# Twelve buffers in place of six for the expert blocks' results

## What is computed

```
gates = softmax(xf @ router_w);  top_v, top_i = top_k(gates, 2)
masked = top_v placed at top_i, divided by its sum
routed[e] = silu(rmsnorm(xf) * rms_w[e] @ w1[e]) @ w2[e]       # e = 0..13, 128 -> 256 -> 128
out = x + sum_e masked[:, e] * routed[e] + two shared experts of the same shape
```

## Time and profile before

| | us |
|---|---|
| median of 3 runs | 412.38 (411.79 to 412.67) |
| profiled execution, its own time | 412.95 |
| its span, first to last instruction | 411.2 |
| POOL's first send of the expert blocks begins | 261.4 |
| SP starts the first load of the results | 391.5 |

### The profile page before, as it was taken

One profiled execution on the slowest core, in us unless ns is written; L12 is line 12 of the kernel. 1 busy time (PEld: TensorE's weight loads), 2 busy tenths in 40 slices (PEclk: granted clock), 3 DMA queues, 4 the chain that ended last, 5 costly groups with the idle time before them and its releaser, 6 DMA issues.

```text
span 411.2 us, 9224 instructions
## 1 busy us (share of the span) xinstructions
PE 281.8 (69%) x2810; PEld 248.4 (60%) x2810; DVE 222.1 (54%) x837; ACT 167.3 (41%) x339; POOL 174.6 (42%) x231
## 2 busy tenths in 40 slices
PE   1945765559666768556656499969797879779800
PEld 1944654558454646354556398969686869678700
DVE  7999977972376455735653041353434343434374
ACT  1466486756485335543541132432323233232300
POOL 2793000008006447445647300355565655646540
PEclk9995798969996598889857599999999998999965
DMA  6750089997000111011102132122222232222289
GB/s 172 254 239 0 17 232 262 266 328 194 0 2 32 33 40 47 32 33 47 40 32 66 60 78 54 33 74 73 72 65 73 63 78 66 77 68 72 65 305 307
DMA packets 54577, 41.67 MB, mean 101 GB/s; under 512 B 6248, under 2 KB 50941, under 8 KB 54033
## 3 DMA queue, kind: packets, MB, share of 16 engines
q1 hardware_dynamic: 47552, 31.60, 26.8%
q0 software_dynamic: 4544, 8.47, 6.5%
q10 hardware_dynamic: 2448, 1.20, 1.1%
HBM read 29.14 MB, written 13.02 MB: 103 GB/s over the span
## 4 chain that ended last, share of the span: by engine, by line
PE 25%; DVE 25%; another core or an unknown queue 16%; issue 12%; DVEq 7%; DMA 5%; ACT 5%; SPq 4%; ACTq 0%
PE bank L1493 4%; DVEq L960 4%; PE bank L1581 3%; PE bank L1592 3%; PE bank L1474 2%; DVE u L698 2%; PE bank L1370 2%; PE bank L1416 2%; DVE area L980 2%; DMA area<-kp_dram 2%; ACT v L1059 2%; PE bank L1293 2%; PE bank L1306 1%; DVE stats L649 1%
## 5 line engine op out<-in xcount | busy, mean ns | idle before, releaser
L588 POOL DMA_INDIRECT y_dram<-area,ybi x78 | 77.9, 998 | 87.8 <-DVE area L980 70.5
L582 POOL DMA_INDIRECT xs_dram<-area x64 | 63.0, 984 | 64.5 <-issue 39.3
L961 DVE COPY v<-v 128x512 f32 x84 | 37.1, 441 | 31.0 <-issue 31.0
L1581 PE MATMUL bank<-xn,v 128*128 128x128 f32 x320 | 44.6, 282 | 3.5 <-DVE v L961 1.8
L1592 PE MATMUL bank<-v,xn 128*128 128x128 f32 x312 | 42.6, 281 | 5.4 <-ACT xn L1240 5.4
L1581 PEld LDWEIGHTS bank<-xn,v 128*128 128x128 f32 x320 | 38.9, 192 | 7.6 <-DVE v L961 4.0
L1592 PEld LDWEIGHTS bank<-v,xn 128*128 128x128 f32 x312 | 38.8, 195 | 6.4 <-DVE area L980 5.2
L1240 ACT ACTIVATE xn<-bank 128x512 f32<-128x512 f32 x40 | 24.1, 602 | 33.0 <-PE bank L1581 20.1
L979 DVE COPY ybi<-area 128x2 uint32<-128x2 uint32 x39 | 7.0, 181 | 54.6 <-remote 40.0
L1235 ACT COPY xn<-bank 128x256 f32<-128x256 f32 x41 | 15.1, 371 | 45.5 <-remote 25.0
L1474 PE MATMUL bank<-v 128*128 128x128 f32 x160 | 26.5, 313 | 9.2 <-issue 9.2
(11 more groups left out here) (298 smaller groups left out, 641.6 us busy)
## 6 DMA issues: line engine op xcount, KB each, us to landing
area<-kp_dram SPq DMA_DIRECT2D x12, 512.0 KB, 6.8
area<-xs_dram SPq DMA_DIRECT2D x84, 65.0 KB
area<-y_dram SPq DMA_DIRECT2D x8, 512.0 KB, 7.6
x_sb<-in_L_attn_x SPq DMA_DIRECT2D x4, 512.0 KB, 8.0
area<-ab_dram SPq DMA_DIRECT2D x2, 1024.0 KB, 6.1
xn<-ab_dram SPq DMA_DIRECT2D x2, 1024.0 KB, 10.9
xn<-kp_dram SPq DMA_DIRECT2D x4, 512.0 KB, 6.8
out_x<-x_sb SPq DMA_DIRECT2D x8, 256.0 KB, 6.5
```

Of the source, the lines that this page charges most:

```text
L582: pool.indirect_dma_start(out=xs_dram.ap(), out_offset=bass.IndirectOffsetOnAxis(ap=pos[:, k, i:i + 1], axis=0), in_=hx[:, i, k, :], in_of ...
L588: pool.indirect_dma_start(out=y_dram.ap(), out_offset=bass.IndirectOffsetOnAxis(ap=ybi[:, z:z + 1].bitcast(U32), axis=0), in_=yb[:, z, :], ...
L961: v.tensor_copy(wc[:, z % STEP], v1_flat.rearrange("p (w m) -> p w m", w=2)[:, :, bass.ds(r, HID)]).then_inc(wc_ready, 1)
L1581: last = mm(bank[2 + p % 2][:, HID * j + P * c:HID * j + P * c + P], wc[:, (2 * p + j) % STEP, 1, P * c:P * c + P], xsT[:, p % 3, P * j:P ...
```

## The change

`yb`, `ybi`, `yb_out`, `last_of` and `ltab` get UNROLL = 12 entries in place of six. `yb` and `ybi` move to a free part of the tensor `u`. POOL's sends take the slots in turn over twelve. DVE's expert loop becomes six pairs written out, a loop of five rounds of six pairs, and three pairs written out, again 39; from pair 6 on it waits for the sends of pair n - 6 (66 waits for 33 pairs). The additions of the shared experts stay at the same pairs. SP reads twelve values of `ltab` in three calls of four in place of six in one, and waits for twelve semaphores; at its end it waits for all twelve again.

```diff
-        yb = area[:, 11032:11032 + STEP * D].rearrange("p (z c) -> p z c", z=STEP)
+        yb = u_flat[:, 1088:1088 + UNROLL * D].rearrange("p (z c) -> p z c", z=UNROLL)
-        ybi = sb("ybi", [P, STEP])
+        ybi = u_flat[:, 2640:2640 + UNROLL]
-        last_of = sb("last_of", [P, STEP])
-        ltab = sb("ltab", [P, STEP], U32)
+        last_of = sb("last_of", [P, UNROLL])
+        ltab = sb("ltab", [P, UNROLL], U32)
-        yb_out = [sem(f"yb_out{z}") for z in range(STEP)]
+        yb_out = [sem(f"yb_out{z}") for z in range(UNROLL)]
             sp.wait_ge(ltab_ready, 1)
-            _, written = nc.values_load_multi_w_load_instructions(
-                ltab[0:1, 0:STEP], engines=[mybir.EngineType.SP], min_val=16 * (ROUTES // P // STEP), max_val=16 * (NBLK // STEP))
+            written = []
+            for z in range(0, UNROLL, 4):
+                written += nc.values_load_multi_w_load_instructions(
+                    ltab[0:1, z:z + 4], engines=[mybir.EngineType.SP], min_val=16 * (ROUTES // P // UNROLL),
+                    max_val=16 * (LOOPS + 1))[1]
             for z, r in enumerate(written):
                 sp.wait_ge(yb_out[z], r)
...
-            for z in range(STEP):
-                sp.wait_ge(yb_out[z], 16 * (NBLK // STEP))
+            for z in range(UNROLL):
+                sp.wait_ge(yb_out[z], 16 * (LOOPS + (z < STEP)))
...
-                    send_block(z % STEP)
+                    send_block((STEP + z) % UNROLL)
...
             def finish_pair(q, p):
-                row, z = 2 * p % UNROLL, 2 * p % STEP
+                row = z = 2 * p % UNROLL
...
+            def finish_again(q, p, sent):
+                for j in range(2):
+                    dve.wait_ge(yb_out[2 * p + j], sent)
+                finish_pair(q, p)
+
+            for p in range(STEP):
+                finish_pair(p, p)
+                if p == STEP - 1:
+                    add_looped(SH_FIRST)
+            with dve.Fori(0, LOOPS - 1) as it:
+                for p in range(UNROLL // 2):
+                    finish_again(it * (UNROLL // 2) + (STEP + p), p, it * 16 + 16)
+                    if p % 3 == 2:
+                        add_looped(it * SH_LOOP + (SH_FIRST + 1 + p // 3))
             for p in range(STEP // 2):
-                finish_pair(p, p)
-            with dve.Fori(0, LOOPS) as it:
-                for p in range(UNROLL // 2):
-                    for j in range(2):
-                        dve.wait_ge(yb_out[(2 * p + j) % STEP], it * (16 * UNROLL // STEP) + 16 * (1 + (2 * p + j) // STEP))
-                    finish_pair(it * (UNROLL // 2) + (STEP // 2 + p), STEP // 2 + p)
-                    if p % 3 == 2:
-                        add_looped(it * SH_LOOP + (SH_FIRST + p // 3))
+                finish_again((LOOPS - 1) * (UNROLL // 2) + STEP + p, p, 16 * LOOPS)
+            add_looped(NT - 1)
```

More of the change, by code:

```diff
@@ L946, in _ @@
             v.tensor_scalar(btab[0:1, :], bank[1][0:1, 2 * P:2 * P + LOADS], float(NULL), None, ALU.min)
-            v.tensor_scalar(last_of[0:1], iota_e[0:1, 0:STEP], cnb[0:1, E - 1:E], -1.0 / STEP, ALU.subtract, ALU.mult)
+            v.tensor_scalar(last_of[0:1], iota_e[0:1, 0:UNROLL], cnb[0:1, E - 1:E], -1.0 / UNROLL, ALU.subtract, ALU.mult)
             v.drain()
             v.engine_nop().then_inc(btab_ready, 1)
-            v.tensor_scalar(last_of[0:1], last_of[0:1], (STEP - 1) / STEP - 0.5 + 1.0 / (2 * STEP), MAGIC, ALU.add, ALU.add)
+            v.tensor_scalar(last_of[0:1], last_of[0:1], (UNROLL - 1) / UNROLL - 0.5 + 1.0 / (2 * UNROLL), MAGIC, ALU.add, ALU.add)
             v.drain()
```

## The result

The changed kernel takes 415.23 us, the median of 14 runs, against 412.33 us of the kernel before, also 14 runs. The ratio is 1.0059, with a 95% interval from 1.0035 to 1.0083: slower by 2.4 us (2.9 by the medians). Forecast were 414.8 us and +0.6%.

The account below looks back on a forecast made before the run. The prediction took the loop to be bound by PE's news arriving behind POOL's bursts of sends, not by landings, and SP's end to be on the path. 2.74 - 0.49 + 0.19 = +2.44; 412.38 + 2.4 = 414.8 us, range 412.3 to 416.9.

Parts of the forecast that it names:

- The waits: DVE before a pair's first instruction: the 40.0 us unknown wait is for PE's product, so twelve slots give 0 us.
- The estimate of 349.6 us: Landing of pair 24's second send, by the skill's DMA figures: 2.3 us before DVE asked for it.
- the order in the chain: Before line 979 on DVE: both landing waits were passed when the 2.63 us unknown wait began.
- ScalarE's simultaneous release: ACT, which waits for nothing from POOL's sends, was released at 354.68, 0.02 us ahead of DVE, after 4.77 us.
- the 21 ns: DVE's first landing wait, line 990: 21 ns in all 36 executions, taken to show that it never held.
- The rival from the semaphore rule: DVE's loop: PE's news costs only 56 ns, so landings held DVE; 21 us less in the loop, 393.8 us; chance 6%.
- SP's end: Between last row loads and first result load: two more calls 2.74, smaller first call -0.49, six more waits 0.19; +2.44 us.
- 1.5 to 3.5: Allowed growth in us from SP's last row load to first result load; outside it the end's price is wrong.
- Nothing hidden behind it: After SP's first result load: loads, additions and stores form one chain, so a later start moves everything, lengths unchanged.
- DVE's longer code and the other slots: DVE's 15 written-out or looped pair bodies (9 before), other buffer places and POOL's slot order: 0 us.
- Rival 4: Expert loop: bursts fall otherwise, winning or losing up to 3.9 us; faster, 410.9, 4%; slower, 418.7, 4%.

Follow-up runs that it names:

- the second pair of profiles: The unchanged kernel before and the changed twelve-slot kernel, both run again on chip 12: 413.66 and 414.07 us by the medians, ratio 1.0043.
- half of the sends: Kernel before, with POOL sending only each pair's even block and the waits for the odd block's landing left out; chip 12, one run: 380.18 us.
- the long end: SP's twelve values in three calls and twelve waits, as in the change; alone on the six-buffer kernel before, chip 11: 415.80 against 412.67 us, ratio 1.0095.
- early reading: SP's table reading moved ahead of its loop, chip 11: kernel before (six buffers) 410.01 us, ratio 0.9938; changed kernel (twelve) 411.65 us, 0.9960.
- sends to nowhere: Kernel before, every result row number out of bounds, so POOL executes all sends and no result is written; chip 12, one run: 412.19 us.

## Why the prediction was right

- *The waits.* Right: DVE's unknown waits aren't waits for landings. The change left them as they were (40.0 and 40.7 us, in the second pair of profiles 37.1 and 44.8), half of the sends removed them, and by the recorded times the landings came 2.3 us or more ahead of DVE's wait. The estimate of 349.6 us for the landing of pair 24's second send was good: its last semaphore update is at 349.59. Of the three reasons given, the order in the chain and ScalarE's simultaneous release were good ones, the 21 ns weren't.
- *The rival from the semaphore rule* of the Trainium skill ("TensorE: Matmul & The Clock Gate", "The cost: per-tile semaphore tail") fell: 56 ns doesn't hold while POOL works off sends; the news came 4 us late in the earlier trace rows. On chip 10 it came at most 0.02 us after the end of PE's row (which is modelled), so there is no such lateness there.
- *SP's end.* The sum was +2.44; the stretch grew by 2.0 and 2.8 us. The mechanism was right, all of it SP's own work on the path. The total was right with its parts uneven. In the first profile the table took 1.6 us more (2.25 forecast) and the waits 0.8 more (0.19 forecast), since one of the 0.7 us pauses fell among them, and the rows' DMAs gave back 0.4. The sum took the two pauses in the old table load as given and put none into what was added, because the new loads don't come right behind DMA starts. That reason doesn't hold: pauses fall on any instruction while POOL sends (last section). Their number differs from run to run, four, seven and nine in the stretches of 9.8, 10.5 and 11.9 us. Growths of 2.0, 2.8 and 4.1 us in three profiles with the long end mean that hitting +2.4 to the tenth was luck; the third lies outside the prediction's own 1.5 to 3.5.
- *Nothing hidden behind it.* Right: the rest is 19.2 to 19.9 us in every full kernel, whenever it starts.
- *DVE's longer code and the other slots.* Priced at 0, and the loops of the twelve-slot kernels (121.3 to 122.0) lie among those of six (120.6 to 122.6). In the times this is known only to about 1 to 2 us, from the two kernels with early reading.
- *Rival 4*, other bursts, wasn't seen: the changed kernel's loops are 0.5 and 1.3 us shorter, its sends mostly in bursts of four. But times scatter for another reason than the loop. The changed kernel's 14 runs lie between 412.93 and 419.26. Its first profile had lost 4.7 of its 5 us by 122.6 us, before POOL's first DMA of rows (125.6), where its granted clock was 0.80 against 0.90 (50 to 100 us) and 0.86 against 1.00 (100 to 125 us). A single run can't tell 2.4 us.

## What to carry to other kernels

Before giving a stage more buffers, find out from the order of its waits which of them ends last: here the one behind the buffers' wait had the whole 40 us. Read it from when each wait's record starts, not from how long it is. Here each register read and semaphore wait at a hand-over between two stages is on the path, 0.25 us a value and 0.7 when the queue pauses; values that are known earlier belong in registers earlier. With that alone this kernel was 0.6% faster than it was (0.2 to 1.1% by the interval), of which the shorter stretch explains half. A bound that seems to be nobody's is worth halving suspects for: half of one engine's instructions showed 31 us at once.

## What the runs showed of the hardware that I had not expected

- The same kernel takes 347.0 us on one chip and 412 to 414 on three other occasions (two other chips, 11 and 12, and the first measurement). On the first of these, chip 10, no unknown wait is in the profiles at all, and the loop takes 91 to 92 us in place of 122; the rest of the 65 us lies mostly ahead of the loop, where the first pair is written at 227 to 231 us in place of 260 to 266. Half of the sends brings the loop of the other kind to the same 91.3. So on three of the four occasions TensorE's news to other engines was held up while GpSimd's indirect DMAs ran in dense sequence, and on chip 10 it wasn't. The kernel with early reading of six values on chip 10, the same 80 us window of the loop:

```profile
229.00:309.00 80.00, 78.35 (x698) 77.65 (x697) 45.01 (x130) 34.20 (x71) 59.57 (x61) 1.00 0.36 95
```

PE is busy there for 78.4 us of 80 with POOL at 59.6, more than the 46.3 beside which PE had 66.0. What differs between the chips isn't known, and only one chip of the faster kind was met.

- The number of slots matters by the kind of chip: four cost 1.1 to 2.3% on chip 10, where the loop is 95.8 us in place of 91 to 92, and landings are named for 19.3 us.
- Instructions of SP's queue pause for about 0.7 us each, whatever they are, and this too goes with POOL's sends. While the sends run, the queue of the kernel before has 80 pieces of 0.60 to 0.76 us (records or gaps between them). Only 3 of them lie more than 1 us away from a burst, where 101 of the queue's 451 instructions lie. With sends to nowhere there are 71, with half of the sends 7, and on chip 10 at most 2, each time with as many DMA starts on SP. Moved work doesn't take the pause along.
